# The dense weight's scale and both fp16 parts made in the first FFN, kept outside the core and loaded at the end of QKV, instead of made in attention

## What is computed

```python
x = x + 0.5 * ffn(layernorm(x), w1, mean_w1, w2, mean_w2, w3, mean_w3)
x = x + attn(layernorm(x), w_qkv, b_qkv, w_dense, b_dense)
x = x + 0.5 * ffn(layernorm(x), ...)

# attn: 32 query heads over 8 key/value heads, head size 16
qkv = einsum('bsh,oh->bso', hidden, w_qkv) + b_qkv
...
probs = softmax(where(mask, scores, min), axis=-1)
ctx = einsum('bhqk,bkhd->bqhd', probs, v).reshape(B, S, 512)
out = einsum('bsh,oh->bso', ctx, w_dense) + b_dense
```

## Time and profile before

| | |
|---|---|
| time, median of 3 runs | 1526.37 us (1523.14 to 1528.73) |
| the profiled execution | 1523.47 us, of which its span 1521.7 |
| PE busy | 1428.3 us, 94% of the span |
| DVE busy | 865.0 us, 57% |
| ACT busy | 601.9 us, 40% |
| POOL busy | 167.8 us, 11% |
| first FFN | to about 489 us |
| QKV | to about 571 us |
| attention | to about 990 us |
| second FFN | to the end |

### The profile page before, as it was taken

How to read it: one execution, slowest core, us unless ns; L and a number is a source line. 1 busy time by engine, 2 the same in 40 slices (tenths; PEclk the granted TensorE clock), 3 DMA queues, 4 the chain that set the end, 5 groups by cost and what they waited for, 6 DMA issues and landing times.

```text
span 1521.7 us, 24288 instructions
## 1 busy us (share of the span) xinstructions
PE 1428.3 (94%) x9136; PEld 628.1 (41%) x9136; DVE 865.0 (57%) x1362; ACT 601.9 (40%) x852; POOL 167.8 (11%) x251
## 2 busy tenths in 40 slices
PE   1999999999999993799999999999999999999998
PEld 0444444444444451233333333334444444444443
DVE  7998414413453766899998999945412412412212
ACT  5862112212221452477777778753212112112111
POOL 1000000000000650233332222210000000000000
PEclk9999999999999995699999999999999999999999
DMA  9605500000000013011112111024000000000000
GB/s 387 224 0 191 234 0 1 0 0 1 1 0 1 1 30 75 1 31 27 28 28 61 26 28 26 2 98 194 0 0 0 28 0 1 28 0 1 28 0 28
DMA packets 64136, 68.88 MB, mean 45 GB/s; under 512 B 52016, under 2 KB 52016, under 8 KB 63536
## 3 DMA queue, kind: packets, MB, share of 16 engines
q1 hardware_dynamic: 64048, 67.67, 13.1%
HBM read 40.63 MB, written 15.20 MB: 37 GB/s over the span
## 4 chain that ended last, share of the span: by engine, by line
PE 88%; DVE 4%; issue 3%; SPq 2%; DMA 1%; ACT 1%; POOL 0%; DVEq 0%; ACTq 0%; POOLq 0%
PE ps L1504 38%; PE ps L1525 17%; PE ps L1743 9%; PE ps L1657 6%; PE ps L1724 5%; PE ps L1644 4%; PE ps L1841 3%; PE ps L1551 2%; PE ps L1498 1%; PE ps L1753 1%; DVE rowmax L1332 1%; DMA w_raw<-w1t 1%; PE ps L1661 1%; SPq L403 1%; SPq L399 1%
## 5 line engine op out<-in xcount | busy, mean ns | idle before, releaser
L803 ACT ACTIVATE probs<-ps 128x1024 f32<-128x1024 f32 (+3 forms) x384 | 292.2, 812 | 85.1 <-PE ps L1724 83.5
L1504 PE MATMUL ps<-xt_hi,w_all 128*128 128x512 f16 x896 | 275.3, 380 | 9.3 <-DVE w_all L1011 9.3
L1332 DVE TENSOR_REDUCE rowmax<-ps 128x2 f32<-128x1024 f32 (+3 forms) x208 | 237.4, 1142 | 12.4 <-PE ps L1665 5.9
L1657 PE MATMUL ps<-ka,qa 48*128 48x512 f16 (+3 forms) x768 | 162.6, 347 | 36.8 <-DVE rowmax L1332 22.6
L1166 DVE SCALAR_TENSOR_TENSOR hb<-ps,scal,silub 128x512 f32<-128x512 f32 x56 | 42.0, 750 | 267.4 <-PE ps L1504 267.4
L1504 PE MATMUL ps<-xt_lo,w_all 128*128 128x512 f16 x448 | 170.5, 381 | 0.0
L1743 PE MATMUL ps<-probs,vs 128*32 128x512 f32 (+3 forms) x1536 | 165.4, 502 | 2.4 <-ACT ctx_sb L822 2.4
L1336 DVE TENSOR_REDUCE rowmax<-ps 128x1 f32<-128x512 f32 x192 | 131.1, 683 | 8.1 <-PE ps L1657 8.1
L1504 PEld LDWEIGHTS ps<-xt_hi,w_all 128*128 128x128 f16 (+1 forms) x896 | 87.9, 98 | 115.1 <-issue 11.4
L1724 PE MATMUL ps<-qa,ka 50*128 50x512 f16 (+3 forms) x768 | 131.8, 331 | 3.2 <-DMA qa<-mrow 2.3
L1525 PE MATMUL ps<-w32b_all,hhib 128*128 (+1 forms) x448 | 133.3, 379 | 0.0
(11 more groups left out here) (164 smaller groups left out, 2090.5 us busy)
## 6 DMA issues: line engine op xcount, KB each, us to landing
spill<-w_all SPq DMA_DIRECT2D x1, 10752.0 KB, 29.0
w32b_all<-spill SPq DMA_DIRECT2D x1, 7168.0 KB, 20.7
x<-x_in SPq DMA_DIRECT2D x4, 1024.0 KB, 5.4
y_out<-x SPq DMA_DIRECT2D x4, 1024.0 KB, 4.2
wbase<-m1t SPq DMA_DIRECT2D x4, 896.0 KB, 12.8
w_raw<-w1t SPq DMA_DIRECT2D x4, 896.0 KB, 14.4
wbase<-m3t SPq DMA_DIRECT2D x4, 896.0 KB, 24.5
w_raw<-w3t SPq DMA_DIRECT2D x4, 896.0 KB, 24.4
```

The costliest lines, as they stand in the source:

```text
L803: nc.scalar.activation(probs[u % PBUF][:, 2 * pair:2 * pair + 2, 0:q1 - q0], wide(("scores", g, (u, pair)))[:, :, 0:q1 - q0], ACT.Exp, sca ...
L1332: nc.vector.tensor_reduce(dst, src, AX.X, ALU.max).then_inc(pair_taken, 1)
L1504: last = mm(ps[:, bank, :], w[a][:, k, bass.ts(t, P)], xt[b][:, k, :], start=(k == 0 and n == 0), stop=(k == HB - 1 and n == 2))
L1657: return mm(ps[:, bank, off:off + w], qa[g % BUF][64 * b:64 * b + ROWS, j, qt * P:(qt + 1) * P], ka[g // 2 % BUF][64 * b:64 * b + ROWS, k0 ...
```

## The change

The dense weight is loaded right behind the QKV weight, early in the first FFN, into free space. Its largest magnitude is taken by DVE beside that of the QKV weight; one POOL reduction (maximum, two columns) serves both. The scale (`dense_units`) follows `qkv_units`, the high part follows that of QKV on ACT, the low part (`dense_low`, now on DVE, one operation) follows `bias_rows`. SP stores both parts to DRAM (`spill_d`) and, at the end of QKV, behind group 3's operands, loads them to their final place, the bias behind them. What attention did for it is gone. The core of the diff:

```diff
         sp.dma_start(bq[:, :], b_qkv.partition_broadcast(P)).then_inc(tables_loaded, 16)
+        sp.dma_start(wd_raw[:, :].rearrange("p (t n) -> p t n", t=HB), wdt.rearrange("(t p) n -> p t n", p=P))\
+            .then_inc(wd_loaded, 16)
+        sp.wait_ge(wdhi_ready, 1)
+        sp.wait_ge(wdlo_ready, 1)
+        sp.dma_start(spill_d.ap(), wd_all[:, :, :, :].rearrange("p s a b -> p (s a b)")).then_inc(wd_spilled, 16)
...
-        sp.dma_start(wd_raw[:, :, :], wdt.rearrange("(t p) n -> p t n", p=P)).then_inc(wd_loaded, 16)
-        sp.dma_start(bd[:, :], b_d.partition_broadcast(P)).then_inc(wd_loaded, 16)
         sp.wait_ge(qkv_full, TOKEN_TILES)
         sp.wait_ge(qkhi_ready, 2 * TOKEN_TILES)
         sp.wait_ge(kpad_ready, 4 + TOKEN_TILES)
         place_operands(3)
+        sp.wait_ge(wd_spilled, 16)
+        sp.dma_start(wd_all[:, :, :, :].rearrange("p s a b -> p (s a b)"), spill_d.ap()).then_inc(dense_loaded, 16)
+        sp.dma_start(bd[:, :], b_d.partition_broadcast(P)).then_inc(dense_loaded, 16)
...
-            if g == 7:
-                sp.wait_ge(wdlo_ready, HB)
-                for i in range(2):
-                    for n in range(2):
-                        sp.dma_start(wd[i][:, 2 * n:2 * n + 2, :], wd_at[2 * i + n][:, :, :]).then_inc(wd_placed, 16)
...
-            if k == 0:
-                dense_bound()
-            if k == 1:
-                for n in range(HB):
-                    dense_low(n)
+            if k == 2:
+                pool.wait_ge(dense_loaded, 32)
...
+                    act.wait_ge(wd_unit, 1)
+                    nc.scalar.activation(wd[0][:, :, :].rearrange("p a b -> p (a b)"), wd_raw[:, :], ACT.Copy,
+                                         scale=wdc[:, 3:4]).then_inc(wdhi_ready, 1)
...
-            if k == 0:
-                dense_magnitude()
...
-            if k == 0:
-                dense_high()
...
-            nc.vector.memset(part[:, 3, 0:1], 0.0).then_inc(part_ready, 1)
+            dve.wait_ge(wd_loaded, 16)
+            nc.vector.tensor_reduce(part[:, 3, 0:1], wd_raw[:, :], AX.X, ALU.max, apply_absolute_value=True)\
+                .then_inc(part_ready, 1)
...
+        def dense_units():
+
+            chain(nc.vector.tensor_copy(wdc[:, 1:2], allr[:, 3, 0:1]))
+            power_of_two(wdc)
+            nc.vector.tensor_tensor(out=scal[:, 4:5], in0=wdc[:, 4:5], in1=wc[:, 4, 4:5], op=ALU.mult).then_inc(wd_unit, 1)
+
+        def dense_low():
+
+            dve.wait_ge(wdhi_ready, 1)
+            nc.vector.scalar_tensor_tensor(
+                out=wd[1][:, :, :].rearrange("p a b -> p (a b)"), in0=wd_raw[:, :], scalar=wdc[:, 3:4],
+                in1=wd[0][:, :, :].rearrange("p a b -> p (a b)"), op0=ALU.mult, op1=ALU.subtract).then_inc(wdlo_ready, 1)
...
                         qkv_units()
+                        dense_units()
...
                         bias_rows()
+                        dense_low()
...
-            if k == 0:
-                dense_scale()
```

More of the change, by code:

```diff
@@ L190, in build @@
     scal = at("scal", [P, 8], F32, K0 + 2528)
+    wdc = at("wdc", [P, 6], F32, K0 + 2432)
     rec = at("rec", [P, 4, Q_PER_KV], F32, K0 + 2560)
@@ L224, in build @@
     ctx_sb = at("ctx_sb", [P, 512], F32, B0 + 32768)
-    wd_raw = at("wd_raw", [P, HB, HID], F32, R0)
-    wd_at = [at(f"wd_at{i}", [P, 2, HID], F16, a) for i, a in enumerate((D0 + 6144, D0 + 14336, B0 + 30720, C0 + 6144))]
-    wd = [at(f"wd_{n}", [P, HB, HID], F16, R0 + 4096 * i) for i, n in enumerate(("hi", "lo"))]
+    wd_raw = at("wd_raw", [P, HB * HID], F32, B0 + 24576)
+    wd_all = at("wd_all", [P, 2, HB, HID], F16, R0)
+    wd = [wd_all[:, i, :, :] for i in range(2)]
     bd = at("bd", [P, HID], F32, R0 + 8192)
@@ L246, in build @@
     spill = nc.dram_tensor("spill", [P, 6 * W_T // 2], F16)
+    spill_d = nc.dram_tensor("spill_d", [P, 2 * HB * HID], F16)
     def sem(name):
@@ L487, in over_partitions @@
             nc.gpsimd.partition_all_reduce(allr[:, w, 1:2], part[:, w, 1:2], P, RMAX).then_inc(allr_ready, 1)
-        for w in range(4):
+        for w in range(3):
             over_partitions(w)
+        pool.wait_ge(part_ready, 4)
+        nc.gpsimd.partition_all_reduce(allr[:, 3, :], part[:, 3, :], P, RMAX).then_inc(allr_ready, 1)
         H2 = HEAD // 2
@@ L782, in _ @@
         act.wait_ge(spilled, 16)
+        act.wait_ge(wd_spilled, 16)
         for i in range(TOKEN_TILES):
@@ L822, in take_context @@
             nc.scalar.copy(ctx_sb[:, :], ps[:, CTX_BANK, :]).then_inc(ctx_ready, 1)
-        def dense_magnitude():
-            act.wait_ge(wd_loaded, 32)
-            nc.scalar.activation(probs[0][:, :, :].rearrange("p h q -> p (h q)"),
-                                 wd_raw[:, :, :].rearrange("p t n -> p (t n)"), ACT.Abs,
-                                 accum_out=part[:, 3, 1:2]).then_inc(part_ready, 1)
-        def dense_high():
-            act.wait_ge(wd_scaled, 1)
-            act.wait_ge(part_ready, 5)
-            nc.scalar.activation(wd_raw[:, :, :].rearrange("p t n -> p (t n)"),
-                                 wd_raw[:, :, :].rearrange("p t n -> p (t n)"), ACT.Copy, scale=wc[:, 3, 3:4])\
-                .then_inc(wd_unit, 1)
-            act.wait_ge(wd_unit, 1)
-            for n in range(2):
-                nc.scalar.copy(wd_at[n][:, :, :], wd_raw[:, 2 * n:2 * n + 2, :]).then_inc(wdhi_ready, 1)
         act.reg_load(score_unit, es[0:1, 0:1].bitcast(I32))
@@ L971, in difference, with power_of_two @@
                                     op=ALU.subtract).then_inc(diff_ready, 1)
-        def power_of_two(w):
-            bound, e, s, inv = (wc[:, w, i:i + 1] for i in (1, 2, 3, 4))
-            tmp = wc[:, w, 5:6]
+        def power_of_two(row):
+            bound, e, s, inv, tmp = (row[:, i:i + 1] for i in (1, 2, 3, 4, 5))
             chain(nc.vector.tensor_scalar(bound, bound, 2.0 ** -30, None, ALU.max))
@@ L1437, in _ @@
         context_low(1)
-        dve.wait_ge(wd_scaled, 1)
+        dve.wait_ge(wd_unit, 1)
         add_dense(0)
@@ L1835, in project @@
             if i == 0 and q == 0:
[L1836 removed]
+                pe.wait_ge(dense_loaded, 32)
             if q == 0:
```

25 lines of the change are left out of this document (6 added, 19 removed).

## The result

The changed kernel takes 1510.01 us, the median of 4 runs (1508.81 to 1511.17), against 1526.86 for the kernel before (4 runs, 1523.14 to 1528.73). The ratio is 0.9893, with a 95% interval of 0.9872 to 0.9913, so 16.3 us less (13.3 to 19.5). The forecast was 1511.3 us, from a sum of 15.1.

A forecast was written before the change was run, and what follows sets the result against it. PE, busy 94% of the span, was taken as the bound, with recoverable waits mostly where QKV passes into attention. 9.7 + 1.6 + 3.8 - 0 = 15.1 us off the median 1526.37 gave 1511.3 us, range 1505 to 1518.

The forecast's parts named there:

- Part 1: QKV-to-attention passage, period 0: the scale leaves DVE's row of pieces, so piece 17 is reduced 9.7 us earlier.
- Part 2: Period 0's join of maxima: POOL's low part leaves, so two short DVE operations run faster; 1.6 us, bounds 1.3 and 1.8.
- Part 3: Attention, group 8: four copies leave SP's queue ahead of its m rows; 3.8 us, bounds 2.5 and 3.8.
- group 8 is still late: Rival: PE still waits for group 8's m rows, moving the copies gives nothing, 1515.1 us; chance 0.13.
- Part 4: First FFN: the added dense-weight work on DVE and ACT hides beside PE's work; cost 0, bounds 0 and +1.3 us.
- Part 5: End of QKV: group 0's m rows, behind 1.25 MB of new loads, land at 613.8, before PE wants them; cost 0.
- The clock as a rival: Rival, pieces after QKV: without the idle, PE's clock rises sooner, saving at most 4.3 us more, 1507.0 us; chance 0.07.
- the span from the start to the end of QKV is the same within 0.5 us: Sign of a right forecast: everything up to QKV's end takes as long as before, within 0.5 us.

The follow-up runs named there:

- Scale behind the join: Kernel before, with the scale's eight DVE operations moved from between pieces 16 and 17 to behind period 0's join of maxima: 1518.0 us, ratio 0.9952.
- the two POOL experiments: Changed kernel with four POOL operations during period 0's join, subtractions reading SBUF in one, memsets only writing in the other; one profile each, no time given.
- done alone, copies a period later: Kernel before, with only the four copies of the dense weight's parts issued one turn of SP's loop later: 1523.82 us, ratio 0.9981.
- undone alone: Changed kernel, with the load of both weight parts issued as four transfers ahead of group 8's m rows instead of one at QKV's end: 1512.88 us, ratio 0.9912.
- the repeated one: Changed kernel measured again, nothing altered: 1509.7 us, ratio 0.9892; its profiled execution was its slowest, 1513.61 us.
- the fills at their second places: Changed kernel with unread matmuls in periods 0 and 1, including 5 ahead of piece 9 and 9 ahead of piece 24, group 0's m rows first: 1507.39 us.
- fill: Changed kernel with unread matmuls added between QKV and the transposed scores, in periods 0 and 1, SP's order unchanged: 1511.62 us, ratio 0.9899.
- fills moved once more: Changed kernel with m rows first and unread matmuls, now 7 instead of 9 ahead of piece 24, 4 new ahead of period 1's piece 1: 1509.2 us.

## Why the prediction was right

- **Part 1** (9.7 us): 9.71 in the trace. The choice of 0.65 us for a pair of overlapping products, not all three, was the right row: PE starts piece 17's products at 597.31 in the changed kernel and DVE takes them at 597.96. "Scale behind the join" moves the same operations in the kernel before and brings the first transposed scores 10.0 us forward.
- **Part 2** (1.6): 1.75 at the join, at the upper bound of 1.8. The cause, POOL's reads, is shown by the two POOL experiments. By the first transposed scores 0.17 is gone again: parts 1 and 2 together are 11.29 there, predicted 11.3.
- **Part 3** (3.8, with a margin of 0.3 us for group 8): 3.81 in the trace; 2.9 (0.6 to 5.2) when done alone and 3.0 when undone alone. The mechanism is right; that the size is right to a hundredth is luck, since it was read from one execution and two others of kernels with the copies in place paid 5.1 and 1.1. The rival "group 8 is still late" did not come in the first profile; in the repeated one the same wait came at group 10, 1.77 us. So the thin margin was real, but it is not group 8's: waits of 1.1 to 1.8 us came at group 6 or 10 in four profiles of kernels without the copies.
- **Part 4** (0, to +1.3): 0.00 between the marks that enclose the work. The products start 260.97 and 268.58, so 0.6 and 0.4 late after the 0.48 us of this execution are taken off; 0.7 and 0.4 were predicted. The operations took 2.27, 1.99 and 2.35 us where 2.23, 1.90 and 2.27 were worked out.
- **Part 5** (0): SP ended group 3's transposes at 607.7, not 606.2, since QKV ended later; the rows landed from 613.5 to 614.2 (613.8 was predicted) and were wanted at 619.1.
- **The clock as a rival** ("PE's clock rises sooner", down to 1507.0): it did not. PEclk is 0.50 from 581 to 625 in the changed kernel, and returns about as long behind the first transposed scores as before. The bound of 4.3 us for a full clock was of the right size: with the fills at their second places the clock is near 1.00 but for 606 to 609, and some 2 to 3 us of it probably come.
- **What missed:** "the span from the start to the end of QKV is the same within 0.5 us" failed: QKV ended 1.58 us later, 0.49 of them from the start of the first FFN and 1.09 from the clock in QKV, and both differ between executions by that much. The sum against the profiled execution is therefore 2.1 too large (15.1 against 13.0), and 0.3 too large with the 1.77 us put back (14.8). Against the medians (16.3 and 16.5 less) it is 1.2 to 1.4 too small, well inside their intervals; that the forecast of 1511.3 lies within 1.6 us of the medians is in part luck, as the runs of one kernel spread over 5 us.

## What to carry over

Work that is small but sits on a serial passage is worth its whole round trip: 1.4 us of operations cost 9.7, since ACT, POOL and DVE waited for each other in turn. Before work is moved out of such a place, list who is late next, and set each against the moment at which it is wanted: ACT's copy 4.0 us later ("scale behind the join") and SP's rows 3 us behind that copy ("fill") both looked like the next limit, and neither cost anything, because PE wants the rows only behind piece 12 of the next period, some 12 us after the join. A delay is a price only where the trace shows a wait for it. And when one profile is set against another, measure between marks that enclose the edit: the ends of two executions differ by more than the edit for reasons that a third kernel shows to be nobody's.

## What the hardware showed that was not expected

- A DVE operation on SBUF of 0.2 us takes 1.2 us beside a POOL subtraction of 1.26 us. Beside a POOL memset the two with two inputs keep their 0.2, and the one with a single input takes 0.49. DVE's reductions from PSUM keep their 0.68 and 1.22 us.
- The return of PE's clock to 2.4 GHz is not fixed by the work: it came 6.8 us behind the first transposed scores in the kernel before, 7.3 in the changed one, 9.5 in "scale behind the join" and 20 in "copies a period later", where PE was busy 14.69 of 15 us at 0.50 (636 to 651). Nor is the fall: the clock fell behind waits of 1.77, 2.05 and 2.28 us, and stayed at 1.00 behind waits of 1.24, 1.58 and 1.78. Three profiled executions that were among their kernel's slowest (the repeated one, copies a period later, fills moved once more) each hold such a stretch at 0.50, so these falls are likely much of what spreads the runs of one kernel, over 5 us in the changed kernel (1508.6 to 1513.6) and 11 in the kernel before (1521.1 to 1532.3).
- SP takes 1.2 to 1.3 us for most of the transposes that it starts. Those of groups 0 to 3 keep it busy without a pause to speak of up to 608 us, so that it reaches group 0's m rows level with ACT's copy of them (608.66, for 0.26 us, and 608.94). No run was held by that.
